# The experts' loop of a mixture-of-experts layer on one Trainium2 core: down products put first, and products nobody reads placed on TensorE

## What is computed

```python
h = xf @ W_router + b_router
Sm = softmax(h, axis=-1)
G_ek, idx_ek = top_k(Sm.T, k)            # 32 experts, k = 256 tokens for each
tokens = xf[idx_ek]
up = einsum('gjkh,ghf->gjkf', tok_g, W_up) + b_up     # 341 columns, a matrix for 4 experts
act = silu(up)
Eout = einsum('ekf,efh->ekh', act, W_down) + b_down   # a matrix for each expert
weighted = G_ek[..., None] * Eout
y = zeros.at[idx_ek].add(weighted)
```

## Time and profile before

| | |
|---|---|
| median of 3 runs | 1272.03 us |
| the profiled execution, its own time | 1269.29 us |
| its span | 1267.5 us |
| mean granted TensorE clock over the span | 0.924 of full speed |
| busy: PE, DVE, ACT, POOL | 84%, 66%, 53%, 58% of the span |

### The profile page before, as it was taken

The page is one execution under the profiler, slowest core; times in us unless marked ns, Lnnn a source line. Parts: engine busy times, 40 slices in busy tenths (PEclk is TensorE's granted clock), DMA queues, the critical chain, the costliest instruction groups (busy, mean ns, idle before and its releaser), DMA issues. The chain is left out here.

```text
span 1267.5 us, 23241 instructions
## 1 busy us (share of the span) xinstructions
PE 1064.4 (84%) x7477; PEld 938.4 (74%) x7477; DVE 830.8 (66%) x2691; ACT 678.1 (53%) x1749; POOL 733.8 (58%) x1188
## 2 busy tenths in 40 slices
PE   4679999999999999999999999999982267777661
PEld 3569888988988988998898899888871145555451
DVE  5346777787676867877686777876765765654110
ACT  0346756666665665666566566666553534423220
POOL 5356675676476557646655774444441044677774
PEclk9799999999999999999999999999995566789786
DMA  3011001100010101001110110000002012344442
GB/s 101 19 32 26 22 21 32 30 27 26 10 32 26 33 24 32 26 10 28 30 33 12 42 28 10 11 9 20 11 20 67 0 41 51 69 70 84 86 67 23
DMA packets 49084, 42.62 MB, mean 34 GB/s; under 512 B 6728, under 2 KB 44488, under 8 KB 48840
## 3 DMA queue, kind: packets, MB, share of 16 engines
q0 software_dynamic: 18432, 22.04, 9.4%
q1 hardware_dynamic: 30536, 19.13, 5.0%
HBM read 27.51 MB, written 13.63 MB: 32 GB/s over the span
## 5 line engine op out<-in xcount | busy, mean ns | idle before, releaser
L657 PE MATMUL mixed<-v,pT 128*128 128x131 f32 x2560 | 318.8, 276 | 6.6 <-DVE o L920 3.8
L657 PEld LDWEIGHTS mixed<-v,pT 128*128 128x128 f32 x2560 | 300.8, 190 | 9.7 <-issue 6.7
L913 DVE TENSOR_REDUCE neg_max<-scores 128x1 f32<-128x1024 f32 (+1 forms) x192 | 198.8, 1035 | 48.5 <-PE scores L444 48.4
L1150 POOL DMA_INDIRECT gram<-in_emb,ids x192 | 190.1, 990 | 67.7 <-issue 51.2
L1078 ACT ACTIVATE probs<-scores,neg_max 128x1024 f32<-128x1024 f32 (+1 forms) x192 | 186.2, 970 | 46.7 <-DVE neg_max L913 45.1
L1087 ACT ACTIVATE pT<-turned 128x512 f32<-128x512 f32 x219 | 130.0, 593 | 73.5 <-PE turned L638 72.2
L1201 POOL TENSOR_TENSOR zb<-row,gate 128x384 f32<-128x384 f32 x64 | 54.5, 852 | 149.4 <-DVE gate L948 148.5
L638 PE MATMUL turned<-con,probs 128*128 128x128 f32 x876 | 126.6, 274 | 12.7 <-ACT probs L1078 5.8
L1962 POOL DMA_INDIRECT out_h<-yw,slots x64 | 102.4, 1600 | 53.4 <-DVE yw L1811 27.6
L638 PEld LDWEIGHTS turned<-con,probs 128*128 128x128 f32 x876 | 101.0, 141 | 28.6 <-ACT probs L1078 12.6
L1953 POOL DMA_INDIRECT xg<-token_table,slots x64 | 64.6, 1009 | 72.4 <-DVE slots L1791 53.5
(11 more groups left out here) (348 smaller groups left out, 2526.2 us busy)
## 6 DMA issues: line engine op xcount, KB each, us to landing
wd<-in_w_down SPq DMA_DIRECT2D x32, 171.0 KB
token_table<-w SPq DMA_DIRECT2D x16, 320.0 KB
out_h<-h SPq DMA_DIRECT2D x16, 256.0 KB, 2.3
gram<-in_emb,ids POOLq DMA_INDIRECT x192
wu<-in_w_up SPq DMA_DIRECT2D x8, 170.5 KB
w<-in_weights SPq DMA_DIRECT2D x1, 1174.0 KB
xg<-token_table,slots POOLq DMA_INDIRECT x64
out_h<-yw,slots POOLq DMA_INDIRECT x64
```

The costliest lines, as they stand in the source:

```text
L657: last = pe.matmul(mixed[:, 0:C + 3], pT[:, n % 2, j * P:(j + 1) * P], vals[:, 0:C + 3], start=(j == 0), stop=(last_half and j == half * 4 ...
L913: dve.tensor_reduce(neg_max[:, n % 4:n % 4 + 1], scores[:, (n % 2) * S:(n % 2) * S + width], AX_X, ALU.max, negate=True).then_inc(maxed, 1)
L1150: pool.indirect_dma_start(gram[:, t % 4, g, :], None, emb[g], bass.IndirectOffsetOnAxis(ap=ids[:, s, t, g:g + 1], axis=0)).then_inc(gather ...
```

## The change

Five things change, all in `experts`.

1. PE: `down(e)` and the first total now come first in iteration e, `up(e + 1)` after them, then the second total, then `turn(e + 2)`, and after that `sums`, `rows` and the places. The third total stays last.
2. DVE: `weigh(e)` comes between the first count and the first settling, `copy_x(e + 2)` after the second settling.
3. ACT: the second count comes ahead of `silu(e + 1)`.
4. `unread(n, bank)`: n bf16 products of 128 x 256 into a bank of `scores` that nothing reads. 13 of them stand ahead of the loop, and in the iterations e < 14 that hold no group's places 8 (with a triple) or 4 (without). That is 8 each in e = 0, 3, 6 and 11, and 4 each in e = 2, 4, 5, 7, 8, 9 and 12: 60 in the loop.
5. The banks and waits that follow from the new order (`PLACE_BANK`, and waits one expert later or earlier in `sums`, `places_within`, `turn` and `down`).

```diff
-    PLACE_BANK = (2, 3, 1, 0, 1)
+    PLACE_BANK = (2, 3, 0, 1, 0)
...
+    UNREAD_TO = 14
...
+        def unread(n, bank):
+
+            for _ in range(n):
+                pe.matmul(scores[:, bank * 512:bank * 512 + TOPK], ones_bf[:], slot_bf[:], start=True, stop=True)
...
-                    pe.wait_ge(y_v, e)
+                    pe.wait_ge(y_v, e + 1)
...
-                    pe.wait_ge(xt_v, e + 1)
+                    pe.wait_ge(xt_v, e + 2)
...
-            if e - 2 in IN_LOOP:
-                pe.wait_ge(chosen_ok, IN_LOOP[e - 2] + 1)
+            if e - 3 in IN_LOOP:
+                pe.wait_ge(chosen_ok, IN_LOOP[e - 3] + 1)
...
-            if e in IN_LOOP:
-                pe.wait_ge(sums_a, IN_LOOP[e] + 1)
+            if e - 1 in IN_LOOP:
+                pe.wait_ge(sums_a, IN_LOOP[e - 1] + 1)
...
         rank(1)
         sums(1)
+        unread(2, 1)
         rows_before(1)
+        unread(3, 1)
         rows(1)
         places_within(1)
         places_before(1)
         pe.wait_ge(ones_set, 2)
+        unread(4, 1)
         rank(2)
+        unread(2, 1)
         rows_before(2)
         turn(0)
+        unread(2, 1)
         rows(2)
         up(0)
         turn(1)
         for e in range(NE):
+            down(e)
+            totals(rounds_of(e)[0:1])
             if e in TRIPLE_AT:
                 rank(TRIPLE_AT[e])
             if e + 1 < NE:
                 up(e + 1)
             if e in TRIPLE_AT:
                 rows_before(TRIPLE_AT[e])
-            totals(rounds_of(e)[0:1])
+            totals(rounds_of(e)[1:2])
+            if e + 2 < NE:
+                turn(e + 2)
             if e in IN_LOOP:
                 sums(IN_LOOP[e])
-            down(e)
-            totals(rounds_of(e)[1:2])
...
-            if e + 2 < NE:
-                turn(e + 2)
+            elif e < UNREAD_TO:
+                unread(8 if e in TRIPLE_AT else 4, (e + 1) % 2)
             totals(rounds_of(e)[2:])
...
             later_count(first)
+            weigh(e)
             later_settle(first)
             later_count(second)
             if e in TRIPLE_AT:
                 reach(TRIPLE_AT[e])
-            weigh(e)
             later_settle(second)
+            if e + 2 < NE:
+                copy_x(e + 2)
             if e in TRIPLE_AT:
                 find_rows(TRIPLE_AT[e])
             later_count(third)
             if e in IN_LOOP:
                 choose(IN_LOOP[e])
-            if e + 2 < NE:
-                copy_x(e + 2)
             later_settle(third)
...
             if e in TRIPLE_AT:
                 keep_ranks(TRIPLE_AT[e])
+            later_count(rounds_of(e)[1:2])
             if e + 1 < NE:
                 silu(e + 1)
             if e in IN_LOOP:
                 keep_sums(IN_LOOP[e])
-            later_count(rounds_of(e)[1:2])
```

## The result

The changed kernel takes **1257.08 us**, the median of 8 runs (1256.30 to 1265.02), against 1272.03 us of the kernel before in 8 runs (1266.88 to 1273.53). The ratio of the runs is 0.9908, with a 95% interval of 0.9887 to 0.9928: 11.7 us less, between 9 and 14. The forecast was 1256.0. The two medians lie 15 us apart, more than the ratio says, since both kernels' runs come in two clusters, and the medians fall into different ones: of the changed kernel's runs five are at 1256.3 to 1257.2 and three at 1262.3 to 1265.0. The profiled execution is one of the upper three, at 1263.79 us.

A forecast was written before the change was run, and what follows sets the result against it. POOL's pattern of 6.41 us an expert was the floor, with 22.0 us of waiting over it. First scatter -3.0, loop -13.1, unread products +0.1 sum to -16.0: 1256.0 us against the 1272.03 median, range 1250 to 1264.

The forecast's parts named there:

- What bounds the kernel: Experts 0 to 11: POOL's fixed 6.41 us an expert is the floor; 22.0 us over it are waiting, 8.9 stay: -13.1.
- The first scatter: Expert 0: `down(0)` no longer stands behind `up(1)`, so `weigh(0)` and the scatter come earlier: -3.0 us.
- the lower bound of 1.2: First scatter: gain in us left if an unnamed pause, like the 2.61 us one on DVE, catches `weigh(0)`.
- the upper bound of 5.0: First scatter: gain of 3.6 us, plus 1.4 if the 13 products bring the clock up before `up(0)`.
- The plain iteration: `down(e)` to `down(e + 1)` without a triple: 6.05 us at 2.4 GHz, under POOL's 6.41; 8.3 at 1.2 GHz.
- The triples: Iterations with `reach`, `find_rows` and `rank`: 3.4 us more, so 9.5, 3.1 over POOL's pattern, which the change leaves.
- The bound of 3.5 us: Experts 0 to 11: what stays over POOL's pattern with no 1.2 GHz stretch and `reach` partly hidden (-18.5).
- The unread products: The 60 in the loop fit PE's waits of 3.2 and 1.6 us and cost nothing; the 13 ahead cost 0.1.
- The clock: PE's granted clock in the loop's first part: a mean near 0.9 in place of 0.69, through the unread products.
- The clock that stays at 0.69: Rival: order moves, clock does not; plain iterations 7.4 us, triples' 10.9, in all 1267.5 us; chance 0.12.
- the slower one: Rival: `weigh` in the search's chain, PE nearly always at 1.2 GHz; iterations 8.3 and 11.7 us, 1276 us; chance 0.06.
- POOL's pattern got longer: Rival: scatters wait for landings or slow beside DVE, eleven times 0.6, +7 us, 1263 us; chance 0.08.

The follow-up runs named there:

- 16 and 8: The changed kernel with 16 unread products in a triple's loop iteration and 8 in others, in place of 8 and 4: 1233.6 us against 1256.43, ratio 0.9829.
- 12 and 6: The changed kernel with 12 unread products in a triple's loop iteration and 6 in others: 1252.32 us against 1272.51, ratio 0.9857.
- 40 and 20: The changed kernel with 40 unread products in a triple's loop iteration and 20 in others: 1243.01 us, ratio 0.9920.

## Why the prediction was right, step by step

**The size.** 1256.0 lies 1 us beside the median, which flatters it: the sum was -16.0, and the ratio makes it -11.7, the traces' loop -12.2. Of the 3.8 us between sum and traces, 1.3 are the part up to the first scatter (with the 0.1 for the 13 products), 1.6 the part up to expert 11, and 0.9 what comes behind.

**What bounds the kernel.** POOL's pattern was the floor, and what the change could win was the 22.0 us over it. 10.4 stayed, 8.9 were forecast. The places were right as well: 3.5, 2.8 and 2.35 us over the pattern at experts 1, 4 and 7 (3.1, 2.7 and 2.3), 0.5 at 10 (0.8). What was not foreseen are 0.5 us at expert 5, behind the iteration of 8.25 us that follows a triple, 0.7 at expert 11, a landing, and 0.87 more behind expert 11, where the scatters' idle time by landings went from 10.9 to 11.6 us.

**The first scatter** was the term that was mis-sized: -1.63 us, against -3.0. The reserve kept for an unnamed pause was right in kind, since just such a pause of 2.7 us came, and the lower bound of 1.2 held. That the pause would come was not known, only that one had, so this part is luck. But the upper bound of 5.0 had left out POOL: its gathers allow 3.9 us at most (24.72 - 20.85). The view that would have shown it, POOL's idle time ahead of the first scatter, 3.94 us, was in the text and was not used as a bound; less the usual 0.30 it gives 3.6.

**The plain iteration**: 5.74 us measured, 6.05 in the sum, under the pattern as said. That the order alone shortens nothing was wrong in its wording: in plain steps POOL's pattern hides it at full clock, but alone it won 6.1 us, with the clock going from 0.72 to 0.80. How much of the 6.1 is the clock's no run separates.

**The triples.** The total came out right with a wrong share in it. I put 3.4 us down to `reach`, `find_rows` and `rank`, which made the iteration 9.5 us and left 3.1 over the pattern as the chain's own. It took 8.78 us (e = 3), and with the clock full 0.9 of its step is left over the pattern (7.3 against 6.4, with two plain iterations' slack of 0.7 each before it). The rest was PE at 1.2 GHz in the iteration behind the gap, 8.25 us where the sum had 6.05. Two errors, a chain put too long with too little slack before it, and a low clock left out of the middle of the sum, nearly cancelled at experts 4 and 7; that the number held there is luck. The bound of 3.5 us for a full clock throughout was near what 16 and 8 products show: 75.06 - 70.5 = 4.6.

**The unread products** cost nothing in their waits, as said, and the waits (2.9 and 1.5 us; I had 3.2 and 1.6) hold more of them. A product of 256 columns takes 112 ns at 2.4 GHz in the trace. The Trainium skill ("TensorE: Matmul & The Clock Gate", Back-to-back issue gap) puts the gap between two isolated products at N / 2.4 + 2.5 ns for that clock, an estimate of 256 / 2.4 + 2.5 = 109 ns here; the trace agrees. At 1.2 GHz (granted clock 0.50 over this row), PE's timeline of the changed kernel ahead of the loop:

```profile
1029.62 1.06 PE L1500 MATMUL scores<-slot_bf,ones_bf 128*128 128x256 bf16 x4
```

That is 0.27 each with the last one's end in it, under the 0.30 that I had taken as a bound. The 13 ahead of the loop cost about 0.1 us, as the sum had it, and the 1.4 us that the early clock was to save measured 1.6, in three of the six profiled executions of the new order that have them.

**The clock** was expected near 0.9 and was 0.88. That the triples' gaps would pull it down was right; that this cost 6 us, and that two more products in a plain iteration and four more in a triple's would save them, I had only as the far end of a range.

**The rivals.** The clock that stays at 0.69 fell with the profile, and so did the slower one, whose plain iterations were all to take 8.3 us (5.74 at full clock; 8.25 only behind a triple). POOL's pattern got longer by landings, some 1.4 us, not 7; a scatter takes 1.62 us as before, beside the search and without it. Such a lockout as the Trainium skill describes ("SBUF — State Buffer", Who interferes with whom) does not show in these rows. No run tests it: one gather ahead of the loop took 1.48 us in place of 0.95, beside DVE's masks and its copy of `xT`, and what lengthened it stays open.

## What to carry to other kernels

Find the engine whose pattern no edit of this kind can shorten, and count each step's excess over it: that is all there is to win, and it names the steps. Where TensorE waits in a chain, unread products in the wait can pay through the clock, as long as they end inside it. Read the wait's length from the trace and vary the number. Here 8 and 4 left a third of what 16 and 8 won between experts 0 and 11, 12 and 6 won as much as those within 0.4 us, and 40 and 20, longer than the waits, gave more than half of it back.

## What was not expected of the hardware

- PE's granted clock went from 0.72 to 0.80 when the same products were put in another order, with PE's busy share hardly changed (65.19 of 86.43 us against 68.45 of 92.50).
- The same 13 products ahead of the loop brought `up(0)` to full clock in five executions (1.55 us) and not in three (2.44, 2.82 and 2.91 us).
- What waits for one product can start 2.4 us behind that product's end in the profile, DVE and SyncE within 0.01 us of each other. On one kind of chip this delay was 0.24 to 2.43 us in four executions, on the other 0.02 or 0.03 us in eight.
- The same attention code begins its fourth maximum at 88.5 or at 95.5 us. The search then begins 6.7 us apart, and most of that stays to the end.
